# Transforms of a Hyena kernel: from 128 by 16 to 64 by 32 points, with half-array matmul pairs

## The reference

```
p    = layernorm(x) @ in_proj_w + in_proj_b          # (8, 2048, 512, 3)
v    = conv3(p[..., 0]) + short_b                    # 3 taps along tokens, per channel
h    = gelu(gelu(pos @ fw1 + fb1) @ fw2 + fb2) @ fw3 + fb3
conv = irfft(rfft(v, 4096) * rfft(h[:, :, 1], 4096), 4096)[:2048]
x    = x + (p[..., 2] * conv) @ out_w + out_b        # p[..., 2] is the gate
out  = x + mixed_adapter(layernorm(x))               # 8 of 32 matrices, 512 by 512, by weight
```

## Time and profile before

| | us |
|---|---|
| median of 3 runs | 2708.38 |
| profiled execution, first to last instruction (span) | 2708.2 |
| TensorE busy | 2570.4 (95%) |
| VectorE busy | 1723.3 (64%) |
| ScalarE busy | 1289.9 (48%) |
| GpSimd busy | 1304.6 (48%) |
| HBM moved | 495.89 MB, 183 GB/s over the span |

### The profile page before, as it was taken

How to read it: one execution, slowest core, us unless ns; L and a number is a source line. 1 busy time by engine, 2 the same in 40 slices (tenths; PEclk the granted TensorE clock), 3 DMA queues, 4 the chain that set the end, 5 groups by cost and what they waited for, 6 DMA issues and landing times. The chain is left out here.

```text
span 2708.2 us, 38386 instructions
## 1 busy us (share of the span) xinstructions
PE 2570.4 (95%) x11252; PEld 1859.0 (69%) x11252; DVE 1723.3 (64%) x2429; ACT 1289.9 (48%) x2021; POOL 1304.6 (48%) x1446
## 2 busy tenths in 40 slices
PE   7679999999999999799999997899999999999999
PEld 2268888888888888433333332788888888888887
DVE  5834434343443434477777776788888888888886
ACT  6634444444444444599999997222222222222222
POOL 1422222222222222366666664676767767776775
PEclk8889999999999999999999999999999999999999
DMA  6533443444344343777777776665555555555553
GB/s 207 171 121 117 183 167 132 158 155 159 119 180 170 128 164 139 263 248 259 263 254 252 249 252 227 233 212 171 169 165 170 170 161 172 169 165 170 169 166 124
DMA packets 233303, 495.89 MB, mean 183 GB/s; under 512 B 20299, under 2 KB 37004, under 8 KB 220244
## 3 DMA queue, kind: packets, MB, share of 16 engines
q1 hardware_dynamic: 181012, 394.39, 43.4%
q10 hardware_dynamic: 52224, 100.68, 9.9%
HBM read 275.58 MB, written 219.43 MB: 183 GB/s over the span
## 5 line engine op out<-in xcount | busy, mean ns | idle before, releaser
L1114 POOL TENSOR_TENSOR m_m<-m_zs,m_spec 128x512 f32<-128x512 f32 x256 | 345.2, 1353 | 240.7 <-ACT m_zs L1070 218.0
L776 POOL TENSOR_TENSOR vl<-v,vh 128x512 fp32r<-128x512 f32 x128 | 165.3, 1291 | 469.7 <-ACT vh L728 469.7
L1029 PE MATMUL m_psW<-m_u,mats 128*128 128x512 f32 x512 | 283.4, 636 | 48.8 <-DVE m_u L1143 48.1
L1143 DVE TENSOR_TENSOR m_u<-m_m 128x512 f32<-128x512 f32 x256 | 269.4, 1062 | 90.2 <-POOL m_m L1114 51.2
L1070 ACT ACTIVATE m_zs<-m_psZ 64x512 f32<-64x512 f32 x512 | 302.5, 591 | 22.1 <-DVE m_m L1131 9.1
L880 DVE COPY fs1o<-psS 128x512 f32<-128x512 f32 x128 | 88.5, 691 | 334.6 <-PE psS L201 334.6
L1305 ACT ACTIVATE b_z<-b_y,b_shift,b_rstd 128x512 f32<-128x512 f32 x128 | 104.3, 815 | 376.0 <-POOL b_shift L1269 376.0
L728 ACT ACTIVATE vh<-v 128x512 fp32r<-128x512 f32 x128 | 80.9, 632 | 401.7 <-DVE v L859 401.7
L1330 PEld LDWEIGHTS b_psC<-b_s,b_fin 128*128 128x128 f32 x2048 | 249.9, 193 | 23.6 <-DMA b_fin<-spec 12.9
L1330 PE MATMUL b_psC<-b_s,b_fin 128*128 128x128 f32 x2048 | 250.9, 276 | 12.5 <-DMA b_fin<-spec 12.5
L1018 PE MATMUL m_psZ<-m_xin,mats 128*128 128x512 f32 x512 | 256.7, 594 | 0.0
(11 more groups left out here) (128 smaller groups left out, 5894.4 us busy)
## 6 DMA issues: line engine op xcount, KB each, us to landing
m_xin<-spec SPq DMA_DIRECT2D x31, 2304.0 KB, 13.2
spec<-fs1o SPq DMA_DIRECT2D x64, 1024.0 KB, 5.8
spec<-m_wo ACTq DMA_DIRECT2D x64, 1024.0 KB, 7.0
b_fin<-spec SPq DMA_DIRECT2D x128, 512.0 KB, 3.7
xg<-in_L_attn_x_dram SPq DMA_DIRECT2D x32, 1024.0 KB, 4.8
gate_t<-gto SPq DMA_DIRECT2D x32, 1024.0 KB, 4.3
b_gin<-gate_t SPq DMA_DIRECT2D x128, 256.0 KB, 3.6
b_xin<-in_L_attn_x_dram SPq DMA_DIRECT2D x128, 256.0 KB, 3.8
```

Of the source, the lines that this page charges most:

```text
L776: pool.tensor_tensor(vl[:, t % 2], v[:, t % 2], vh[:, t % 2].bitcast(F32), ALU.subtract).then_inc(v_lo, 1)
L1029: pe.matmul(psW[k][:], kind(INV, i, t), u[:, (t % GB - 1) % R, :], start=True, stop=True).then_inc(w_ps, 1)
L1114: pool.tensor_tensor(m2[:, b % R, :], zs[:, b % R, :], spec[:, par, 1, :], ALU.mult).then_inc(m2_done, 1)
L1143: dve.tensor_tensor(u[:, b % R, :], m1[:, b % R, :], m2[:, b % R, :], ALU.add).then_inc(u_done, 1)
```

## The change

The split of the 2048 points becomes 64 by 32. A token's number is n = 32 p' + 16 h + t: partition h*64 + p' of tile t. There are still 16 tiles per batch, 32 groups of 128 spectrum rows, and 4096 rows per batch in each spectrum. What changes:

- **Step 1** (front): the contraction is over 64 tokens, so one tile holds two independent transforms, on partitions 0 to 63 and 64 to 127. Each gives 128 rows. The six matmuls have 64 rows of weights in place of 128, and alternate between the two halves of the array. ScalarE copies both results with one instruction of 128x1024; VectorE copies none. The preparation does the same in float32, with two matmuls of 64 rows.
- **Step 2** (middle): one float32 matmul with 64 rows for each half of the partitions, into two banks. The matrix has twice the columns, so the second 64 hold the result with real and imaginary part exchanged.
- **Product**: one VectorE instruction of 128x1024, PSUM times spectrum. The copies with exchanged halves, the work of GpSimd and the sum are gone; the sum is made by step 3.
- **Step 3**: for each batch two float32 matmuls of 64 output rows and 128 rows of contraction, one for each half of the output partitions. Two batches are done together (`PAIR_AT`), and ScalarE copies them out with one instruction of 128x1024.
- **Step 4** (back): two float32 matmuls of 64 output rows by 512 columns with the matrix as weights; the result has tokens on the partitions. The output projection needs channels there, so four transposes `turn_o` are added before it, into a new bank `b_psP`, of which ScalarE and VectorE make the high and low parts.
- **Gate**: in token order, by 12 matmuls of the same size for each tile, with its bias added on VectorE (`g_bias`) in place of ScalarE.
- **Preparation**: the running sum is taken once, of `h2` before its last layer (128x2048), and the last layer is applied to the sums per tile (`sums`: two matmuls of 64 output rows and one of 64 rows for the bias). `filter_rows` with channels on partitions, its copies, three of four scans and the eight 128x2048 copies are gone; one multiplication on VectorE (`e1`) per tile is added.
- The lists of the back are reordered on TensorE, ScalarE and VectorE; `b_psT` goes from two banks to one.

```diff
 # front
+                    for half, h in ((lo, 0), (hi, 1)):
+                        pe.matmul(psS[:, h, :], s1h[half, t, :], vh[half, t % 2, :], start=True, stop=False)
+                    for half, h in ((lo, 0), (hi, 1)):
+                        pe.matmul(psS[:, h, :], s1h[half, t, :], vl[half, t % 2, :], start=False, stop=False)
+                    for half, h in ((lo, 0), (hi, 1)):
+                        mm = pe.matmul(psS[:, h, :], s1l[half, t, :], vh[half, t % 2, :], start=False, stop=True)
-                pipelined(pe, B, N2, [(turn, 2), (project_v, 3), (project_x2, 6), (stage1, 4)])
+                pipelined(pe, B, T, [(turn, 2), (project_v, 3), (project_g, 3), (stage1, 4)])
 # middle
+                    pe.matmul(psA[k % RA][:, 0, :], w[0:R2], src[0:R2], start=True, stop=True)
+                    mm = pe.matmul(psA[k % RA][:, 1, :], w[R2:P], src[R2:P], start=True, stop=True)
+                    for k in range(2):
+                        pe.wait_ge(m_done, n + k + 1)
+                        pe.matmul(psW[0:R2, k, :], back_first if first else back_w, m[:, (2 * pair + k) % RM, 0, :], start=True, stop=True)
+                        pe.matmul(psW[R2:P, k, :], back_w, m[:, (2 * pair + k) % RM, 1, :], start=True, stop=True).then_inc(w_ps, 1)
-                pipelined(pe, GROUPS // 2, T, [(stage2, 0), (stage3, 4)])
+                pipelined(pe, GROUPS // 2, S, [(forward, 0), (inverse, 4)])
+                    dve.tensor_tensor(m[:, (k - 1) % RM], psA[k % RA][:], spec[:, par], ALU.mult).then_inc(m_done, 1)
 # back
-                    for ct in range(CT):
-                        for j in range(2):
-                            mm = pe.matmul(psC[t % 2][:, ct * P:(ct + 1) * P], fin[:, t % 2, j, ct * P:(ct + 1) * P],
-                                           s4[:, j, t, :], start=(j == 0), stop=(j == 1))
+                    for h in range(2):
+                        mm = pe.matmul(psC[t % 2][h * N1:(h + 1) * N1, :], s4[:, h * T + t, :], fin[:, t % 2, h, :], start=True, stop=True)
+                def turn_o(b, t):
+                    pe.wait_ge(o_done, no(b, t) + 1)
+                        mm = pe.transpose(psP[:, ct * P:(ct + 1) * P], o[:, t % 2, ct * P:(ct + 1) * P], ident[:])
-                pipelined(pe, B, N2, [(conv, 1), (project, 2), (turn, 3), (adapt, 4)])
+                pipelined(pe, B, T, [(conv, 1), (adapt, 4), (turn_z, 3), (turn_o, 1), (project, 2)])
-                pipelined(dve, B, N2, [(finish, 5), (bias_x, 0), (gate, 1), (o_low, 1), (residual, 2), (z_low, 3)])
+                pipelined(dve, B, T, [(bias_x, 0), (gate, 1), (finish, 4), (z_low, 3), (o_low, 1), (residual, 2)])
```

More of the change, by code:

```diff
@@ L123, in stage_matrices, with beside, over @@
     cross_sp[:, :, :, 0] = 0.0
[L125 to L132, removed]
+    R = 2 * N2
+    def beside(x, y):
+        return np.concatenate([x.reshape(R, R), y.reshape(R, R)], axis=1)
+    def over(x, y):
+        return np.concatenate([x, y], axis=0)
+    data, data_sp = beside(fwd, fwd[:, :, ::-1]), beside(fsp, fsp[:, :, ::-1])
+    filt, filt_sp = beside(same(fwd), cross(fwd)), beside(same_sp, cross_sp)
+    back, back_sp = inv.reshape(R, R), isp.reshape(R, R)
+    mid = np.concatenate([over(data_sp, data), over(filt_sp, filt), over(data, data), over(filt, filt),
+                          over(back_sp, back_sp), over(back, back)], axis=1)
+    t_, h_, n_ = np.meshgrid(np.arange(T), np.arange(2), np.arange(N1), indexing="ij")
+    ramp = (n_ * N2 + h_ * T + t_ + 1) / BR
     return {
         "pos": np.linspace(0.0, 1.0, L).astype(np.float32).reshape(1, L),
-        "s1": in_groups(s1.reshape(N1H, N2, ROWS), 2).astype(np.float32),
-        "s1x": in_groups(s1x.reshape(1, ROWS), 1).astype(np.float32),
-        "s4": in_groups(s4.reshape(ROWS, N2, N1H), 0).astype(np.float32),
+        "ramp": ramp.astype(np.float32).reshape(1, L),
+        "s1": s1.reshape(N1, 2, T, ROWS).transpose(1, 0, 2, 3).reshape(P, T, ROWS).astype(np.float32),
+        "s1x": s1x.reshape(1, ROWS).astype(np.float32),
+        "s4": s4.reshape(ROWS, N2, N1).astype(np.float32),
         "mid": mid.astype(np.float32),
@@ L140, in stage_matrices, with by_tile @@
     }
[L143 to L147, removed]
+def by_tile(rows):
+    return rows.rearrange("(n h t) c -> h n t c", h=2, t=T)
 def pipelined(eng, outer, tiles, stages):
@@ new lines, in sums, with stage1 @@
+                def sums(t):
+                    if t >= 2:
+                        pe.wait_ge(e1_done, t - 1)
+                    for h in range(2):
+                        cols = cum[:, t + h * T:t + h * T + (N1 - 1) * N2 + 1:N2]
+                        pe.matmul(pE[t % 2][h * N1:(h + 1) * N1, :], cols, w3s[:], start=True, stop=False)
+                    pe.matmul(pE[t % 2][:], ramp_r[:, t * P:(t + 1) * P], b3hl[:], start=False, stop=True).then_inc(c_ps, 1)
+                def stage1(t):
+                    edge_row = t == T - 1
+                    pe.wait_ge(g_done, t + 1)
+                    if t >= 2:
+                        pe.wait_ge(s1_out, t - 1)
+                    for h in range(2):
+                        half = slice(h * N1, (h + 1) * N1)
+                        end = not (edge_row and h == 1)
+                        mm = pe.matmul(pS[t % 2][:, h, :], s1[half, t, :], g[half, t % GR, :], start=True, stop=end)
+                    if edge_row:
+                        pe.wait_ge(before_done, 1)
+                        mm = pe.matmul(pS[t % 2][:, 1, :], s1x[:], g_before[:], start=False, stop=True)
+                    mm.then_inc(s1_ps, 1)
@@ L1002, in stage2 @@
                             pe.wait_ge(x_in[par], 16 * (i + par))
[L1003 to L1004 removed]
+                            pe.wait_ge(m_done, n - 1)
+                    else:
                         if first:
[L1006 to L1009 removed]
@@ new lines, in store @@
+                def store(i, s):
+                    if PAIR_AT.get(s % GB, 0) % 2 == 0:
+                        return
+                    par, pair = s // GB, PAIR_AT[s % GB]
+                    batches = slice(2 * pair - 2, 2 * pair + 2)
+                    act.wait_ge(w_out, group(i, s) * (B // 2) + pair + 1)
+                    act.dma_start(rows_of(spec3, group(i, s))[:, batches], wo[:, par, batches]).then_inc(stored[par], 16)
+                pipelined(act, GROUPS // 2, S, [(spectrum, 0), (out_copy, 4), (store, 4)])
@@ L1145, in _ @@
-                pipelined(dve, GROUPS // 2, T, [(same_part, 0), (product, 2)])
+                    par, k = s // GB, s % GB
+                    n = data_no(i, s)
+                    dve.wait_ge(a_ps, n + 1)
+                    if k == 1:
+                        dve.wait_ge(f_done, group(i, s) + 1)
+                    if not (at_first(i, s) and k <= RM):
+                        dve.wait_ge(w_ps, n - RM + 1)
+                    dve.tensor_tensor(m[:, (k - 1) % RM], psA[k % RA][:], spec[:, par], ALU.mult).then_inc(m_done, 1)
```

757 lines of the change are left out of this document (311 added, 446 removed).

## The result

The changed kernel takes 3310.23 us (median of 4 runs, 3306.74 to 3318.72) against 2709.03 for the kernel before on the same chip: ratio 1.2225, interval 1.2207 to 1.2242. It is slower, far outside the range that was forecast. That 3316 us, the price of the rival "no overlap", lies beside it is chance: the halves overlap perfectly, and the loss is somewhere else.

What follows compares the result with a forecast made beforehand. TensorE's list was taken to bound front and back, that list plus waits the middle, mostly VectorE the preparation. 2708 - 12 (preparation) - 40 (front) + 75 (middle) + 58 (back) = 2789 us, range 2610 to 3020.

Steps and rivals of the forecast that it cites:

- no overlap: Rival, 15%: half-array matmuls never run at the same time; middle 433 us more, back 110, front 50, preparation 15: 3316 us.
- DMA moves the same spectra: Term for transfers: no time added; the middle would ask for 4.3 MB in 19.9 us, less per us than now.
- Middle: Middle group forecast at 19.9 us against 17.58 before, 75 us more over 32 groups.
- half-array queues of their own: Rival, 30% together with cheap switches: each half works through its own records; middle group 16.5 us, total 2620 us.
- In-order issue: Main case, 45%: halves overlap only in program order, n pairs in a row cost (2n+1) x 0.43 us; total 2789 us.
- third case: Rival, 10%: only row halves overlap; step 3 costs 165 us more, step 4 55 us more: 3010 us.
- The chain of waits: Middle: of 3.0 us of waits and small gaps a group, 0.3 stay, most going with the chain over three engines.
- The switch: TensorE changing tile shape: 0.195 us each, bounded by 0.1 to 0.2; eight a group in the middle, 1.6 us.
- Front: Front tile 7.04 us in place of 7.35: step 1 costs 1.09 in place of 1.40, 40 us less.
- Step 4: Back: one isolated pair with its switches, 1.68 us in place of 1.70; 1.25 under the rival of separate queues.
- `turn_o` and the lists: Back: 0.35 us for the new transposes plus 0.1 (0 to 0.5) of waiting per tile, 58 us more.
- Preparation: Preparation: 12 us less (0 to 20), with VectorE at 98 - 13 + 12 us.

Runs made afterwards that it cites:

- e7: Changed kernel with the back's load of x and store of the output each split into two DMAs of 64 partitions: 2762.83 us, ratio 1.0195.
- e8: e7 with the load of x moved to the front of SyncE's list in the back: 2754.32 us, ratio 1.0164.
- e10: e8 with the back's lists on TensorE, VectorE and ScalarE in the order of the kernel before: 2647.57 us, ratio 0.9770.
- e6: Changed kernel with both matmuls of each step 2 pair on the lower half of the array: 3571.94 us.
- e4: Changed kernel with the front's six step 1 matmuls issued three per half in turn in place of alternately: 3322.09 us.
- e2: Kernel before, with only the back's load of x changed to the changed kernel's pattern (outermost dimension 2): 3172.16 us.

## Why the prediction was wrong

**The step that failed** is the sentence on DMA: "DMA moves the same spectra". It priced bytes of the middle and didn't ask how the back's transfers of x and output are laid out after the change, though the diff renames their pattern and the earlier trace rows has the wait `b_xin` of before (16.8 us in all). The term (0 us) measures, from after to e7, 547 us. It has two parts: the landing of 9.4 us in a loop that had 0.5 us of slack, and two narrow transfers a tile that together need some 12 us. The prediction never followed the loop VectorE, SyncE, transfer, VectorE; with 3.8 + 3.4 = 7.2 against 7.72 it was the next bound of the back behind TensorE's list.

**Where the 528 us between the forecast (2789) and the profiled span (3316.9) are.** Back (12.90 - 8.15) x 128 = +608; middle (16.02 - 19.9) x 32 = -124; front +4; the rest (preparation, fills) +40.

**Middle.** The disputed overlap went to the rival "half-array queues of their own" (16.5 forecast, 16.02 measured). In-order issue was the wrong choice between the two. L931 and L932 start together, every 0.43 us:

```profile
1200.78 0.59 PE L945 MATMUL m_psW<-m_m,mats 128*64 128x512 f32 x1
1200.78 0.59 PE L946 MATMUL m_psW<-m_m,mats 128*64 128x512 f32 x1
1201.31 0.69 PE L931 MATMUL m_psA<-m_xin,mats 64*128 64x512 f32 x1
1201.31 0.69 PE L932 MATMUL m_psA<-m_xin,mats 64*128 64x512 f32 x1
1201.84 0.59 PE L931 MATMUL m_psA<-m_xin,mats 64*128 64x512 f32 x1
1201.85 0.59 PE L932 MATMUL m_psA<-m_xin,mats 64*128 64x512 f32 x1
1202.27 0.59 PE L931 MATMUL m_psA<-m_xin,mats 64*128 64x512 f32 x1
```

Whether two column halves run together was the doubt of the third case; L945 and L946 are such, and they do. The chain of waits went as forecast, 3.0 us a group to nothing: what is left of 16.02 after 17 x 0.86 is 8 x 0.175, and the switches alone fill that.

**The switch.** 0.195 was taken. The rows above have 0.53 and 0.53 where 0.43 is normal: 0.20 into the row halves. Into the column halves it is 0.15 (1198.91, 1199.44 and 1199.92 are 0.53 and 0.48 apart). Right within its bounds.

**Front.** 7.04 forecast, 7.07 measured. Right; the bias of the gate and the copy of 1024 columns cost nothing that shows.

**Step 4.** 1.68 was forecast for the pair with its two switches. From the pair's start to the next matmul's it is 1.01 us (2399.46 to 2400.47), with 0.1 more ahead of it and behind the next (distances of 0.33 in place of 0.233), 1.2 in all. That is near the 1.25 of the rival, since the records of this pair overlap too.

**`turn_o` and the lists.** I added 0.1 us for a wait (0 to 0.5), and wrote that a wait over 0.5 would mean that the reordered lists cost more than allowed. They do: with DMA out of the way (e8) 8.73 - 7.67 = 1.1 us a tile are theirs and those of the pauses described under e10. I looked for the wait at `b_o`, where the diff adds an instruction; it came at `b_z`, where the list had moved the cover away. The price of the three reordered lists together, e8 to e10, is 107 us.

**Preparation.** 12 us less forecast, none seen: the front starts at 160.8 against 161.5. The forecast's terms gave VectorE 98 - 13 + 12 = 97 us, hardly less than before. Its busy time did fall, from 98 to 78 in 25 to 143.8 us of both traces, but the time didn't follow; TensorE now waits for `e`, 15.6 us in five waits. No experiment was made on it.

## What to carry to other kernels

Read every transfer's outermost dimension before and after a change of layout, even where bytes and rows stay the same: of 256 KB, 2 cost 9 us, 8 cost 4.5 and 128 cost 3.8. Where an engine list, a queue and a transfer form a loop, add up its round and compare it with the tile, since here half a microsecond of slack was all that stood between no cost and 4 us a tile (12.90 to 8.81). Matmuls on two halves of the array can be counted at half their time each, plus 0.15 to 0.2 us for every change of shape; what a new order of a list costs is read from the longest path between two of its entries, not from what was added.

## What the runs showed of the hardware

- Two halves of TensorE run fully beside each other: row halves in float32 (0.86 us for a pair in the middle, 1.72 when both use one half, e6) and in fp32r, column halves in float32. For row halves in fp32r the order in the program doesn't matter (7.08 against 7.07 us a tile, e4).
- A 256 KB transfer whose outermost dimension is 2 keeps two DMA engines busy at 51 GB/s together; the semaphore gets 2, 8 or 16 increments at landing for outermost dimensions of 2, 8 and 128.
- A narrow transfer slows others that the program doesn't tie to it: in e2 `b_fin` went from 3.7 to 9.3 us.
- TensorE's clock falls with its waits: in the back of the changed kernel the granted clock is 0.85, and behind a wait of 3.18 us for `b_o` the projection's matmuls start 0.43 apart for seven of twelve, where they had 0.233 (the earlier trace rows has that distance at full clock; 0.43 is the lower level, 1.2 GHz). Seven times 0.2 is 1.4 us in this tile, on top of the wait.
- A split transfer is two issues of 0.48 us each in place of one of 0.56 (L1114). SyncE and ScalarE both carry that in e10, where TensorE sets the tile.
- A pause of 7.3 us on VectorE stands at each repetition of its loop over the batches in e10, ahead of the first instruction of the list. In each of the five two transfers of 8 KB of the kind "instruction" run between the loop's branch and that first instruction (1882.6 and 1886.7 us in the pause that ends at 1888.6). The kernel before has no transfer of that kind from 1958 to 2592 us and no such pause. That the pause is the loading of instructions is likely by this, and not tested.
